# Row counts that are multiples of 16 in the transfers of a message-passing kernel, and 60 one-hot blocks in place of 58

## The chip, the cores and the metric

The kernel runs on one core of one Trainium2 chip. The core has a matrix engine (PE, TensorE), a vector engine (DVE), a scalar engine (ACT), GpSimd (POOL), a queue engine (SP) that only issues transfers here, and 16 DMA engines that the queues of SP, ACT and POOL share. The metric is the time of one execution on the device in microseconds, less being better.

## The reference

One layer of a graph network on 12,500 nodes with 32 features and 200,000 edges, the edges sorted by destination. For every edge the source row and the destination row go through a four-layer perceptron; the messages are averaged per destination node, added to x and normalised. The edge attributes are not used.

```
x_j = x[src];  x_i = x[dst]
h = relu(concat([x_i, x_j - x_i]) @ W1 + b1)      # 64 -> 64
h = relu(h @ W2 + b2)                             # 64 -> 128
h = relu(h @ W3 + b3)                             # 128 -> 64
m = h @ W4 + b4                                   # 64 -> 32
s, cnt = segment_sum(m, dst), segment_sum(1, dst) # over 12,500 nodes
out = layernorm(x + s / max(cnt, 1))
```

## The kernel before

The edges are cut into 196 blocks of 1,024 (`S_N`). Each block is one step of a pipeline: PE makes layer 1, ACT applies the relus, PE makes layers 2 and 3, turns the result and sums it into a window of nodes with a one-hot of the destinations that DVE builds. Layer 4 is applied once per node at the end.

The source rows of a block come in one of two ways. In a *gathered* block POOL issues eight indirect transfers of 128 rows each (L564), of rows of x for the first five blocks (`PLAIN`) and of rows of x that layer 1 has already been applied to (`z_rows`) for the others; PE only turns them (L859). POOL runs up to ten blocks ahead (`R`). In a *sorted* block (the first `SB` = 58 blocks of edges) no row is gathered: DVE builds one-hots of the sources (L1270) from lists that SP spreads over the partitions (`load_windows`, L467), and PE picks the rows out of all 12,500 nodes with 113 small matmuls (`selected_x`, L897). Those lists are sorted on DVE before (`merge`, L1143 and L1144), turned into windows by ACT (`window_sources`, L656), stored in DRAM by SP (`store_windows`, L458) and loaded again.

`STEPS` sets the order: 14 gathered steps, then from step 14 on one sorted step and two gathered steps in turn until the sorted blocks are used up (step 185), then gathered steps to the end (186 to 195). SP, ACT, PE and DVE each go through the steps in this order, in a loop of one pass for this input.

Ahead of the steps, in seven groups of 16 node columns (`YG`, `YC`), PE applies layer 1 to all nodes (L790), ACT and DVE split the result (L636, L637, L1062, L642, L1068), and SP stores it in DRAM: `z_rows` (L418) and `y_rows` (L420). The nodes lie as 125 partitions (`NP`) of 100 nodes. The buffers of a group are used again two groups later, so ACT waits at L634 and L635 for the stores of the group before last. POOL's gathers of `z_rows`, and the first step, wait for all of the stores.

Transfers whose partition count is not 128 are: the load of x by ACT (L608, 125 rows), the destinations of the gathered blocks (`dst_i`, L380, 68 rows) and their relative form (L424, `LP` = 69 rows), the stores of `z_rows` and `y_rows` (125), of the three parts of x (`x_rows`, L512, two pieces of 125 rows) that are loaded again as 98 blocks (`load_blocks`, L427), of the windows of sources (L458, 58 rows, eight pieces), the load of x once more for the end (L494, 125 rows), issued in the first step after the last sorted one and used by DVE two steps later (`centre_x`, a quarter of the columns in each of four steps), and the store of the result in eight chunks (L545, 125 rows).

Of the kernel before, what the change touches and what calls it, by code (L numbers as in the profile page):

```python
# [13 lines left out]
N, E = 12500, 200000  # L14
# [14 lines left out]
XP = 3 * D  # L29


SB = 58
HALVES = 64
GB = S_N - SB
B0 = SB * PE2
LP = GB // 2
LC = 2 * PE2
# [13 lines left out]
for n in range(S_N):  # L51
    k = (n - FIRST_SORTED) // PERIOD
# [40 lines left out]
YG = 7  # L93
NP = 125
# [3 lines left out]
CHUNKS = [(0, EDGE)] + [(EDGE + CH * n, CH) for n in range(6)] + [(NC - EDGE, EDGE)]  # L98
LAG = 2
XH = 2  # L100
# [12 lines left out]
def build(nc, x, src, dst, W1, b1, W2, b2, W3, b3, W4, b4, consts, bounds, out):  # L113
# [3 lines left out]
    with ctx:  # L117
# [53 lines left out]
        rel16 = part(region16, 0, (LC,))[0:LP, :]  # L171
        x_nat = part(region, ring, (NC * D,))[0:NP, :]
# [29 lines left out]
        x_parts = part(x_p, 0, (NC, 3, D))  # L202
# [7 lines left out]
        dst_i = part(sums_all, 2 * SBL * T, (LC,))[0:LP, :].bitcast(I32)  # L210
# [11 lines left out]
        z_new = [part(work, n * 5 * UE, (YC, H1))[0:NP, :, :] for n in range(2)]  # L222
        y_new = [part(work[:, :].bitcast(BF16), n * 10 * UE + 4 * UE, (YC, 3, H1))[0:NP, :, :, :] for n in range(2)]
# [66 lines left out]
        s_x2 = sem("x_in_once_more")  # L290
# [61 lines left out]

        def rows_stored(eng, rows):
            for n in range(2):
                eng.wait_ge(rows[n], 16 * len(range(n, YG, 2)))

        def layer3_copied(eng, s):

            if s < AHEAD - 2:
                eng.wait_ge(s_h3a, s + 1)  # L360
            else:
                eng.wait_ge(s_h3c, s + 3 - AHEAD)

        def piece(h):
            return slice(h * NC // XH, (h + 1) * NC // XH)
# [6 lines left out]
        def _(sp):  # L372
# [4 lines left out]
            sp.dma_start(src_i[0:FULL - fb * T, fb, :], tiled[fb * T:FULL, :]).then_inc(s_src, 16)  # L377
            sp.dma_start(src_i[FULL - fb * T:FULL - fb * T + 1, fb, 0:HALF], src[E - HALF:E].unsqueeze(0)).then_inc(s_src, 16)
            body = dst[B0:B0 + (LP - 1) * LC].rearrange("(p e) -> p e", e=LC)
            sp.dma_start(dst_i[0:LP - 1, :], body).then_inc(s_dst, 16)  # L380
            a = E - B0 - (LP - 1) * LC
            lastp = dst_i[LP - 1:LP, :]
            sp.dma_start(lastp[:, 0:a], dst[B0 + (LP - 1) * LC:E].unsqueeze(0)).then_inc(s_dst, 16)
# [31 lines left out]
            for g in range(YG):  # L415
                at, w = slice(g * YC, g * YC + width(g)), width(g)
                sp.wait_ge(s_znew, g + 1)
                sp.dma_start(z_rows.rearrange("(p c) f -> p c f", p=NP)[:, at, :], z_new[g % 2][:, 0:w, :]).then_inc(s_zst[g % 2], 16)  # L418
                sp.wait_ge(s_ylo, g + 1)
                sp.dma_start(y_rows[0:N, :, :].rearrange("(p c) k f -> p c (k f)", p=NP)[:, at, :],  # L420
                             y_new[g % 2][:, 0:w, :, :].rearrange("p c k f -> p c (k f)")).then_inc(s_yst[g % 2], 16)
                if g == 0:
                    sp.wait_ge(s_rel16, 1)
                    sp.dma_start(dst_rows[B0:B0 + LP * LC].rearrange("(p e) -> p e", e=LC), rel16).then_inc(s_dst_st, 16)  # L424
# [50 lines left out]
            def step(s):  # L475
                if is_sorted(s) and STEPS[s] + 1 < SB:
                    for c in range(CN - QN):
                        load_windows(STEPS[s] + 1, QN + c)
                if s + RX < S_N:
                    load_dst(s + RX)  # L480
                    load_rows(s + RX)
                if AHEAD <= s < SSTEP[0] - 1:
                    for c in range(3):
                        if 3 * (s - AHEAD) + c < CN:
                            store_windows(3 * (s - AHEAD) + c)
                if s == SSTEP[0] - 2:
# [9 lines left out]
            sp.wait_ge(s_dst_st, 16)  # L496
            sp.wait_ge(s_ypad, 16)
            rows_stored(sp, s_yst)
            load_first()
            for s in range(AHEAD):  # L500
                step(s)
                if s == 0:
                    sp.wait_ge(s_keys, 1)
                    for n, v in enumerate((bound_lo, bound_hi)):
                        sp.dma_start(v[0:SB, :], bounds[n, :].unsqueeze(0).to_broadcast([SB, PE2])).then_inc(s_bound, 16)
                if s == HALF_STEP:
                    sp.wait_ge(s_half, 1)
                    sp.dma_start(key0[0:SB, 0:UE], key0[HALVES:HALVES + SB, UE:PE2]).then_inc(s_across, 16)
                if s == PARTS_STEP:
                    for h in range(XH):  # L510
                        sp.wait_ge(s_lo, h + 1)
                        sp.dma_start(x_rows[0:N, :, :].rearrange("(p c) k f -> p c k f", p=NP)[:, piece(h), :, :],  # L512
                                     x_parts[0:NP, piece(h), :, :]).then_inc(s_xst, 16)
                if s == PARTS_STEP + 1:
                    sp.wait_ge(s_xst, (XH + 1) * 16)
# [26 lines left out]

            for n, (c0, w) in enumerate(CHUNKS):
                sp.wait_ge(s_y, n + 1)
                sp.dma_start(out.rearrange("(p c) f -> p c f", p=NP)[:, c0:c0 + w, :], zc[:, c0:c0 + w, :]).then_inc(s_out, 16)  # L545
            sp.wait_ge(s_out, 16 * len(CHUNKS))

        @block.gpsimd
        def _(pool):
# [55 lines left out]

        @block.scalar
        def _(act):
            act.dma_start(x_nat, x.rearrange("(p c) f -> p (c f)", p=NP)).then_inc(s_x, 16)  # L608
# [21 lines left out]
            def split_rows(g):  # L630
                for i in range(4):
                    act.wait_ge(s_zy4[i], g + 1)
                if g >= 2:
                    act.wait_ge(s_zst[g % 2], 16 * (g // 2))  # L634
                    act.wait_ge(s_yst[g % 2], 16 * (g // 2))  # L635
# [121 lines left out]
        def _(pe):  # L757
# [34 lines left out]
                        if t == width(g) // 4 - 1:  # L792
                            made.then_inc(s_zy4[i], 1)

            pe.wait_ge(s_x, 16)
            turn_x(0)
            pe.wait_ge(s_w1s, 1)
            for g in range(YG):
# [204 lines left out]
        def _(dve):  # L1003
# [17 lines left out]
                    nc.vector.tensor_copy(src_t[:, a:b], ps[:, k, 0:b - a]).then_inc(s_idx, 1)  # L1021

            def subtract_bases():
                dve.wait_ge(s_dst, 4 * 16)
# [267 lines left out]
            def build_onehot(s):  # L1292
                v, n = s % 2, STEPS[s]
                if s >= 2:
                    dve.wait_ge(s_agg, s - 1)
                if n == 0:
                    dve.wait_ge(s_maskc, 1)
                if s == 0:
                    dve.wait_ge(s_dst_st, 16)
# [66 lines left out]
            with dve.Fori(0, end, WIN) as off:  # L1366
# [3 lines left out]
                for s in range(AHEAD, S_N + 3):  # L1370
# [2 lines left out]
                        copy_masked()  # L1373
                    if SSTEP[-1] + 3 <= s < SSTEP[-1] + 3 + XQ:
                        if s == SSTEP[-1] + 3:
                            dve.wait_ge(s_x2, 16)
# [86 lines left out]
```

## Time and profile before

| | |
|---|---|
| median of 3 runs | 2545.24 us (2544.97 to 2545.98) |
| profiled execution, its own time | 2551.01 us |
| its span | 2549.2 us |
| mean granted TensorE clock | 0.803 |
| PE busy | 1782.1 us (70%) |
| DVE, ACT, POOL busy | 844.8, 634.2, 1093.8 us (33%, 25%, 43%) |
| moved by DMA | 300.61 MB |

Busy time is summed over instructions, and matmuls overlap, so a busy PE is not PE at its peak. "Idle before" in a row of the timeline is the time that the engine stood still ahead of that instruction, and behind the arrow stands what ended it; "remote" there means that the profile does not show who did, "issue" that nothing it shows was waited for.

### The profile page before, as it was taken

The numbers are of one execution on the slowest core, as the hardware profiler recorded it, in microseconds if no ns is written. First come the engines' busy times: TensorE is split into PE (matmuls) and PEld (weight loads), VectorE is DVE, ScalarE is ACT, GpSimd is POOL, SyncE is SP. The second block draws the span as 40 slices with busy tenths as digits, with TensorE's granted clock in tenths as the row PEclk, the third lists the DMA queues.
The fourth block names the chain that finished last, engine by engine and source line by source line (L and its number), as shares of the span: only waits on it lengthen the run. The fifth ranks groups of instructions, "written<-read, shape, count | busy, mean of one in ns | idle before, by whom it ended". The sixth has DMA issues, their size and how long they took to land.

```text
span 2549.2 us, 39560 instructions
## 1 busy us (share of the span) xinstructions
PE 1782.1 (70%) x13928; PEld 1173.7 (46%) x13928; DVE 844.8 (33%) x1777; ACT 634.2 (25%) x999; POOL 1093.8 (43%) x1123
## 2 busy tenths in 40 slices
PE   2133516777787777787777777777877778777887
PEld 2111303555454554555554555554555545555547
DVE  2342602333333333333333333332333333333352
ACT  2222314222222222222222222222222222222241
POOL 4175263444444444444444444444344444444402
PEclk9975756878878788878888878888788888887885
DMA  3221414444434444444444444443444443444310
GB/s 114 81 65 29 114 35 149 142 133 133 132 112 140 137 139 125 126 123 142 139 138 125 127 123 142 136 138 105 128 142 137 139 123 120 131 142 133 93 58 27
DMA packets 194466, 300.61 MB, mean 118 GB/s; under 512 B 83633, under 2 KB 90015, under 8 KB 193697
## 3 DMA queue, kind: packets, MB, share of 16 engines
q1 hardware_dynamic: 158439, 260.74, 32.3%
q0 software_dynamic: 35168, 35.43, 6.7%
q8 instruction: 116, 1.90, 0.3%
q10 hardware_dynamic: 658, 1.85, 0.2%
q14 instruction: 85, 0.70, 0.1%
HBM read 283.89 MB, written 13.87 MB: 117 GB/s over the span
## 4 chain that ended last, share of the span: by engine, by line
PE 41%; another core or an unknown queue 22%; issue 16%; DVE 9%; DMA 5%; ACT 3%; DVEq 3%; SPq 0%; POOL 0%; ACTq 0%; POOLq 0%
PE ps L897 21%; PE ps L921 5%; PE ps L929 3%; PE ps L949 3%; DVEq L1314 3%; PE ps L937 2%; PE ps L841 2%; PE ps L911 2%; PE ps L998 2%; DVE region L1270 2%; DVE region L1301 2%; PE ps L859 1%; DMA dstb<-dst_rows 1%; DMA y_rows<-work 1%
## 5 line engine op out<-in xcount | busy, mean ns | idle before, releaser
L564 POOL DMA_INDIRECT xj<-z_rows,src_t x1059 | 1038.2, 980 | 1293.4 <-PE ps L859 785.6
L897 PE MATMUL ps<-region,x_p 128*96 128x155 bf16 (+51 forms) x6554 | 611.4, 259 | 268.5 <-issue 238.0
L897 PEld LDWEIGHTS ps<-region,x_p 128*96 128x96 bf16 x6554 | 544.1, 162 | 395.4 <-issue 367.3
L1270 DVE TENSOR_SCALAR region<-region,cst 128x1629 bf16<-128x1629 int16 x464 | 274.0, 643 | 348.6 <-remote 295.1
L929 PE MATMUL ps<-work,w3s 128*64 128x512 f32 x784 | 311.5, 697 | 69.0 <-ACT work L683 38.5
L683 ACT ACTIVATE work<-ps,b2s 128x512 f32<-128x512 f32 x392 | 256.8, 685 | 205.7 <-remote 147.0
L1289 DVE COPY work<-ps 128x512 f32<-128x512 f32 x188 | 129.2, 687 | 504.0 <-remote 278.5
L921 PE MATMUL ps<-work,w2s 64*128 64x512 f32 x784 | 252.9, 726 | 45.5 <-ACT work L675 41.1
L690 ACT ACTIVATE work<-ps,b3s 128x512 f32<-128x512 f32 x196 | 134.7, 687 | 529.6 <-remote 468.4
L675 ACT ACTIVATE work<-ps,b1s 128x512 f32<-128x512 f32 x196 | 134.8, 688 | 507.7 <-PE ps L841 363.0
L937 PE MATMUL ps<-cst,work 128*128 128x128 f32 x784 | 138.3, 303 | 139.8 <-ACT work L690 99.3
L1316 DVE TENSOR_TENSOR sums<-sums,ps 65x42 f32 (+1 forms) x334 | 67.7, 203 | 361.3 <-remote 179.0
L952 PE MATMUL ps<-region,work 128*65 128x42 f32 x2208 | 177.3, 248 | 12.4 <-issue 6.6
L952 PEld LDWEIGHTS ps<-region,work 128*65 128x65 f32 x2208 | 175.8, 159 | 12.9 <-issue 11.5
L921 PEld LDWEIGHTS ps<-work,w2s 64*128 64x128 f32 x784 | 65.4, 204 | 237.0 <-ACT work L675 164.8
L937 PEld LDWEIGHTS ps<-cst,work 128*128 128x128 f32 x784 | 89.7, 150 | 178.0 <-ACT work L690 112.4
L664 ACT ACTIVATE work<-ps 96x512 bf16<-96x512 f32 x58 | 34.4, 593 | 491.5 <-PE ps L897 491.5
L929 PEld LDWEIGHTS ps<-work,w3s 128*64 128x64 f32 x784 | 61.4, 150 | 150.4 <-ACT work L683 84.4
L1280 DVE CAST work<-ps 96x512 bf16<-96x512 f32 x58 | 39.8, 687 | 247.5 <-PE ps L897 247.5
L859 PEld LDWEIGHTS ps<-cst,xj 128*128 128x128 f32 x552 | 59.8, 144 | 127.5 <-issue 127.5
L859 PE MATMUL ps<-cst,xj 128*128 128x128 f32 x552 | 93.6, 294 | 20.5 <-DVE work L1233 19.3
L841 PE MATMUL ps<-region,ywin 126*64 126x512 bf16 x508 | 93.1, 400 | 20.8 <-DVE region L1262 11.6
(156 smaller groups left out, 940.2 us busy)
## 6 DMA issues: line engine op xcount, KB each, us to landing
dstb<-dst_rows SPq DMA_DIRECT2D x196, 252.0 KB
region<-src_rows SPq DMA_DIRECT2D x116, 391.2 KB
region<-src_rows SPq DMA_DIRECT2D x58, 407.2 KB
region<-src_rows SPq DMA_DIRECT2D x58, 403.2 KB, 4.8
region<-src_rows SPq DMA_DIRECT2D x58, 376.2 KB
region<-src_rows SPq DMA_DIRECT2D x58, 375.8 KB, 3.7
region<-src_rows SPq DMA_DIRECT2D x58, 374.0 KB
region<-src_rows SPq DMA_DIRECT2D x58, 366.2 KB, 5.4
```

Of the source, the lines that this page charges most:

```text
L564: pool.indirect_dma_start(out=xj[:, u, j % UT, j // UT, 0:w], out_offset=None, in_=rows, in_offset=bass.IndirectOffsetOnAxis(ap=cols[:, j: ...
L675: nc.scalar.activation(h1[:, v, :], p_h1, ACT.Relu, bias=b1s[:, 0:1]).then_inc(s_r1, 1)
L683: nc.scalar.activation(h2[:, v, h, :], p_h2[:, h, :], ACT.Relu, bias=b2s[:, 0:1]).then_inc(s_r2[h], 1)
L690: nc.scalar.activation(h3[:, v, :], p_h3, ACT.Relu, bias=b3s[:, 0:1]).then_inc(s_r3, 1)
L841: added = nc.tensor.matmul(p_h1[h * H1:(h + 1) * H1, :], rows, pick[:, v, k, h * UE:(h + 1) * UE], start=False, stop=k == steps - 1, skip_ ...
L859: turned = nc.tensor.matmul(to[:, t * T:(t + 1) * T], xj[:, u, t, :, :].rearrange("p h f -> p (h f)"), ident, start=t == 0, stop=True, is_ ...
L897: chosen = nc.tensor.matmul(ps[0:XP, XBANK[h], lo - h * UE:hi - h * UE], xb[:, a, :], hot[:, q % QN, at + lo:at + hi], start=not begun[h], ...
L921: nc.tensor.matmul(p_h2[:, h, :], w2s[r:r + H1, :], h1[r:r + H1, s % 2, :], start=True, stop=True).then_inc(s_l2[h], 1)
L929: nc.tensor.matmul(p_h3[h * H3:(h + 1) * H3, :], w3s[:, :], h2[:, s % 2, h, :], start=True, stop=True).then_inc(s_l3, 1)
L937: turned = nc.tensor.transpose(p_ht[:, t * T:(t + 1) * T], h3[:, s % 2, t * T:(t + 1) * T], ident)
L952: summed = nc.tensor.matmul(p_agg[:, h * KN:(h + 1) * KN], h3t[:, v, t, h, :], onehot[:, v, j, 0:KN], start=t == 0, stop=t == UT - 1)
L1270: nc.vector.tensor_scalar(hot[:, q % QN, 0:CW[c]], spread[:, q % QE, 0:CW[c]], cst[:, C_PID:C_PID + 1], None, ALU.is_equal).then_inc(s_hot, 1)
```

## The change

Two things. `SB` goes from 58 to 60: with it the gathered blocks go from 138 to 136, `LP` from 69 to 68, the partitions that hold the sorted blocks from 58 to 60, and steps 188 and 191 are sorted steps. And every transfer of 125, 68 or 67 rows is issued as two: a multiple of 16 rows (112 or 64) and the rest (13, 4 or 3); the semaphore counts follow.

```diff
-SB = 58
+SB = 60
+        def even_rows(n):
+            return slice(0, n // 16 * 16), slice(n // 16 * 16, n)
...
-            sp.dma_start(dst_i[0:LP - 1, :], body).then_inc(s_dst, 16)
+            for rows in even_rows(LP - 1):
+                sp.dma_start(dst_i[rows, :], body[rows, :]).then_inc(s_dst, 16)
...
-                sp.dma_start(z_rows.rearrange("(p c) f -> p c f", p=NP)[:, at, :], z_new[g % 2][:, 0:w, :]).then_inc(s_zst[g % 2], 16)
+                for rows in even_rows(NP):
+                    sp.dma_start(z_rows.rearrange("(p c) f -> p c f", p=NP)[rows, at, :], z_new[g % 2][rows, 0:w, :])\
+                        .then_inc(s_zst[g % 2], 16)
...
-                    sp.wait_ge(s_block, CN * SB)
-                    sp.dma_start(x_nat, x.rearrange("(p c) f -> p (c f)", p=NP)).then_inc(s_x2, 16)
+                    for rows in even_rows(NP):
+                        sp.dma_start(x_nat[rows, :], x.rearrange("(p c) f -> p (c f)", p=NP)[rows, :]).then_inc(s_x2, 16)
```

In the same manner the stores of `y_rows` (L420), of the relative destinations (L424), of `x_rows` (L512) and of the result (L545), and ACT's load of x (L608). The stores of the windows (L458), of the sorted destinations (L519) and the copy L508 are not split; their row count is `SB`. Waits change only in their counts (`2 * 16` for `16`, `5 * 16` for `4 * 16`, `2 * XH + 1` for `XH + 1`).

## Rows read from the trace of the kernel before

**Rows 1.** Stretches: us, busy time of each engine, granted clock, DMA share, GB/s
```profile
10.00:15.00 5.00, 0.00 (x0) 0.00 (x0) 0.00 (x0) 3.42 (x2) 0.00 (x0) 1.00 0.32 133
110.00:115.00 5.00, 0.81 (x8) 0.51 (x8) 2.69 (x3) 3.00 (x3) 0.00 (x0) 1.00 0.32 132
408.00:410.00 2.00, 0.00 (x0) 0.00 (x0) 0.00 (x0) 1.15 (x2) 0.00 (x0) 1.00 0.20 58
414.00:416.00 2.00, 1.08 (x14) 1.11 (x15) 0.65 (x1) 0.00 (x0) 0.00 (x0) 0.50 0.74 296
```

**Rows 2.** Timeline, the start: us, duration, engine, line, what, idle before
```profile
2.03 12.62 SPq L378 DMA_DIRECT2D sums<-in_src  x1
21.65 1.16 ACT L619 ACTIVATE sums<-sums 128x1152 f32<-128x1152 int32 x1 [8.23 <-DMA sums<-in_src]
26.06 1.12 POOL L564 DMA_INDIRECT xj<-in_x,src_t  x1 [24.69 <-DVE src_t L1021]
```

**Rows 3.** Timeline, the groups of node columns and their stores
```profile
77.09 0.94 POOL L564 DMA_INDIRECT xj<-in_x,src_t  x1 [0.30 <-issue]
83.81 1.02 ACT L636 ACTIVATE work<-ps 125x1024 f32<-125x1024 f32 x1 [37.84 <-remote]
91.11 1.02 ACT L636 ACTIVATE work<-ps 125x1024 f32<-125x1024 f32 x1 [3.02 <-PE ps L790]
...
120.06 0.38 ACT L636 ACTIVATE work<-ps 125x256 f32<-125x256 f32 x1 [5.43 <-DMA y_rows<-work]
122.11 0.27 SPq L420 DMA_DIRECT2D y_rows<-work  x1
131.79 0.95 POOL L564 DMA_INDIRECT xj<-z_rows,src_t  x1 [53.75 <-DMA z_rows<-work]
133.51 0.07 DVE L1233 MEMSET work<- 128x16 f32 x1 [11.42 <-DMA y_rows<-work]
```

**Rows 4.** Timeline, the parts of x stored and loaded again
```profile
261.02 1.67 SPq L512 DMA_DIRECT2D x_rows<-x_p  x2
...
281.62 0.85 SPq L427 DMA_DIRECT2D x_p<-x_rows  x1
...
296.60 0.49 DVE L1262 TENSOR_SCALAR region<-dstb,node_off 126x1024 bf16<-126x1024 int16 x1 [2.46 <-DMA dstb<-dst_rows]
```

**Rows 5.** Timeline, the last store of windows and the first load
```profile
402.84 0.24 SPq L458 DMA_DIRECT2D src_rows<-region  x1
...
410.08 4.37 SPq L467 DMA_DIRECT2D region<-src_rows  x8
```

**Rows 6.** Timeline, DVE's one-hots of sorted blocks, POOL's last gather
```profile
445.83 0.84 DVE L1301 TENSOR_TENSOR region<-iota_s,dst_rel 128x672 f32<-128x672 f32 x1
...
2407.45 0.85 DVE L1301 TENSOR_TENSOR region<-iota_s,dst_rel 128x672 f32<-128x672 f32 x1
2408.65 0.95 POOL L564 DMA_INDIRECT xj<-z_rows,src_t  x1 [0.31 <-issue]
2427.30 0.85 DVE L1301 TENSOR_TENSOR region<-iota_s,dst_rel 128x672 f32<-128x672 f32 x1
```

**Rows 7.** Timeline, PE inside one sorted block, and in the last gathered steps
```profile
1500.73 0.68 PE L897 MATMUL ps<-region,x_p 128*96 128x153 bf16 x4 [1.04 <-issue]
1503.59 6.80 PE L897 MATMUL ps<-region,x_p 128*96 128x12 bf16 x69 [0.86 <-issue]
...
2463.67 0.65 PE L859 MATMUL ps<-cst,xj 128*128 128x128 f32 x4
2468.18 0.66 PE L859 MATMUL ps<-cst,xj 128*128 128x128 f32 x4
```

**Rows 8.** Timeline, x loaded once more and its first use
```profile
2424.13 0.28 SPq L494 DMA_DIRECT2D region<-in_x  x1
...
2440.65 0.99 DVE L1320 TENSOR_REDUCE xmean<-region 125x25 f32<-125x800 f32 x1 [7.73 <-DMA region<-in_x]
2441.67 0.18 DVE L1321 TENSOR_SCALAR xmean<-xmean 125x25 f32<-125x25 f32 x1
```

**Rows 9.** SP's waits: line, waited for, us in total, times, longest
```profile
SPq L117 <- DMA out<-region: 6.5, 1, 6.5
```

More of the change, by code:

```diff
@@ L354, in rows_stored @@
             for n in range(2):
-                eng.wait_ge(rows[n], 16 * len(range(n, YG, 2)))
+                eng.wait_ge(rows[n], 2 * 16 * len(range(n, YG, 2)))
         def layer3_copied(eng, s):
@@ L417, in _ @@
                 sp.wait_ge(s_znew, g + 1)
-                sp.dma_start(z_rows.rearrange("(p c) f -> p c f", p=NP)[:, at, :], z_new[g % 2][:, 0:w, :]).then_inc(s_zst[g % 2], 16)
+                for rows in even_rows(NP):
+                    sp.dma_start(z_rows.rearrange("(p c) f -> p c f", p=NP)[rows, at, :], z_new[g % 2][rows, 0:w, :])\
+                        .then_inc(s_zst[g % 2], 16)
                 sp.wait_ge(s_ylo, g + 1)
-                sp.dma_start(y_rows[0:N, :, :].rearrange("(p c) k f -> p c (k f)", p=NP)[:, at, :],
-                             y_new[g % 2][:, 0:w, :, :].rearrange("p c k f -> p c (k f)")).then_inc(s_yst[g % 2], 16)
+                for rows in even_rows(NP):
+                    sp.dma_start(y_rows[0:N, :, :].rearrange("(p c) k f -> p c (k f)", p=NP)[rows, at, :],
+                                 y_new[g % 2][rows, 0:w, :, :].rearrange("p c k f -> p c (k f)")).then_inc(s_yst[g % 2], 16)
                 if g == 0:
                     sp.wait_ge(s_rel16, 1)
-                    sp.dma_start(dst_rows[B0:B0 + LP * LC].rearrange("(p e) -> p e", e=LC), rel16).then_inc(s_dst_st, 16)
+                    for rows in even_rows(LP):
+                        sp.dma_start(dst_rows[B0:B0 + LP * LC].rearrange("(p e) -> p e", e=LC)[rows, :], rel16[rows, :])\
+                            .then_inc(s_dst_st, 16)
             def load_blocks(rows):
@@ L493, in step @@
                     sp.wait_ge(s_block, CN * SB)
-                    sp.dma_start(x_nat, x.rearrange("(p c) f -> p (c f)", p=NP)).then_inc(s_x2, 16)
-            sp.wait_ge(s_dst_st, 16)
+                    for rows in even_rows(NP):
+                        sp.dma_start(x_nat[rows, :], x.rearrange("(p c) f -> p (c f)", p=NP)[rows, :]).then_inc(s_x2, 16)
+            sp.wait_ge(s_dst_st, 2 * 16)
             sp.wait_ge(s_ypad, 16)
@@ L511, in _ @@
                         sp.wait_ge(s_lo, h + 1)
-                        sp.dma_start(x_rows[0:N, :, :].rearrange("(p c) k f -> p c k f", p=NP)[:, piece(h), :, :],
-                                     x_parts[0:NP, piece(h), :, :]).then_inc(s_xst, 16)
+                        for rows in even_rows(NP):
+                            sp.dma_start(x_rows[0:N, :, :].rearrange("(p c) k f -> p c k f", p=NP)[rows, piece(h), :, :],
+                                         x_parts[rows, piece(h), :, :]).then_inc(s_xst, 16)
                 if s == PARTS_STEP + 1:
-                    sp.wait_ge(s_xst, (XH + 1) * 16)
+                    sp.wait_ge(s_xst, (2 * XH + 1) * 16)
                     load_blocks(x_rows[0:NROT, :, :])
@@ L544, in _ @@
                 sp.wait_ge(s_y, n + 1)
-                sp.dma_start(out.rearrange("(p c) f -> p c f", p=NP)[:, c0:c0 + w, :], zc[:, c0:c0 + w, :]).then_inc(s_out, 16)
-            sp.wait_ge(s_out, 16 * len(CHUNKS))
+                for rows in even_rows(NP):
+                    sp.dma_start(out.rearrange("(p c) f -> p c f", p=NP)[rows, c0:c0 + w, :], zc[rows, c0:c0 + w, :])\
+                        .then_inc(s_out, 16)
+            sp.wait_ge(s_out, 2 * 16 * len(CHUNKS))
         @block.gpsimd
@@ L607, in _ @@
         def _(act):
-            act.dma_start(x_nat, x.rearrange("(p c) f -> p (c f)", p=NP)).then_inc(s_x, 16)
+            for rows in even_rows(NP):
+                act.dma_start(x_nat[rows, :], x.rearrange("(p c) f -> p (c f)", p=NP)[rows, :]).then_inc(s_x, 16)
             act.dma_start(cst[:, :], consts).then_inc(s_cst, 16)
@@ L633, in split_rows @@
                 if g >= 2:
-                    act.wait_ge(s_zst[g % 2], 16 * (g // 2))
-                    act.wait_ge(s_yst[g % 2], 16 * (g // 2))
+                    act.wait_ge(s_zst[g % 2], 2 * 16 * (g // 2))
+                    act.wait_ge(s_yst[g % 2], 2 * 16 * (g // 2))
                 nc.scalar.activation(four(z_new[g % 2], g), of_group(slice(0, H1), g), ACT.Copy).then_inc(s_znew, 1)
@@ L793, in make_rows @@
                             made.then_inc(s_zy4[i], 1)
-            pe.wait_ge(s_x, 16)
+            pe.wait_ge(s_x, 2 * 16)
             turn_x(0)
@@ L1023, in subtract_bases @@
             def subtract_bases():
-                dve.wait_ge(s_dst, 4 * 16)
+                dve.wait_ge(s_dst, 5 * 16)
                 nc.vector.tensor_reduce(base_p[:, :], dst_i.rearrange("p (h e) -> p h e", h=UP), AX.X, ALU.min)\
@@ L1298, in build_onehot @@
                 if s == 0:
-                    dve.wait_ge(s_dst_st, 16)
+                    dve.wait_ge(s_dst_st, 2 * 16)
                 nodes, w = (iota_s, WIN) if n < SB else (iota_g, KN)
@@ L1375, in _ @@
                         if s == SSTEP[-1] + 3:
-                            dve.wait_ge(s_x2, 16)
+                            dve.wait_ge(s_x2, 2 * 16)
                         centre_x(s - SSTEP[-1] - 3)
```

## The prediction

> **What bounds the kernel now.** I read the times of stretches first. While a transfer of 125 rows is the only large one, as x in the first microseconds and y at 110, the DMA share stands at 0.32 with 132 to 133 GB/s [rows 1]. 0.32 of 16 engines is five, at 26 GB/s each. With stores of 58 rows the share is 0.20 at 58 GB/s, which is two engines at that rate and a rest of gathers; with loads over 128 partitions it is 0.74 and 296 GB/s, with the ramp inside the stretch [rows 1]. So a transfer seems to be dealt out in equal shares of whole rows: 125 = 5 x 25, 58 = 2 x 29, 128 = 16 x 8. The change turns 125 into 112 = 16 x 7 and 13, 69 into 64 and 4, and, unsaid, every 58 into 60 = 15 x 4.
>
> Then I ask with the timeline where such a transfer ends a wait on the path. The reader is to see six places: the start [rows 2], the groups of node columns [rows 3], the parts of x [rows 4], the windows [rows 5], the second load of x [rows 8] and the end [rows 9]. Between 446 and 2407 us none does. There the time is made by PE's order of steps. From one sorted one-hot to the next but 55 is (2407.45 - 445.83) / 56 = 35.03 us for one sorted and two gathered steps [rows 6]. When POOL has issued its last gather, at 2408.65, the next such period takes 2427.30 - 2407.45 = 19.85 us, and a gathered step alone 2468.18 - 2463.67 = 4.51 us [rows 6, 7]. In the period before, 16 gathers were issued. PE's small matmuls show why: while POOL gathers they come in threes and fours with gaps of about 1 us ("issue"), and after its last gather of the burst 69 of them pass in 6.80 us [rows 7]. A gather thus costs PE about (35.03 - 19.85) / 16 = 0.95 us although PE waits for no data. A gathered block costs 4.51 + 8 x 0.95 = 12.1 us, a sorted one 19.85 - 2 x 4.51 = 10.8 us.
>
> **The change part by part.** The sum is made against the profiled execution's 2551.0 us (span 2549.2), which is 5.8 above the median of the runs; that difference is kept.
>
> (a) Start. ACT's copy of the sources begins at 21.65 after 8.23 us of idle that a load of sources ended; SP stood 12.62 us in the issue of the last of these [rows 2], as long as x (1.6 MB at 133 GB/s is 12.0 us) holds the first five engines. On 16 engines x takes about 4 us. The copy can then start when ACT's own work ends, 8.2 us earlier; everything behind it, POOL's first gather at 26.06 too, moves with it. Value 8.2; bounds 0 (another engine's load is late instead) and 8.2.
>
> (b) The long wait. ACT waits 37.84 us for PE's third group, until 83.81, and POOL's 40th gather ends at 78.03 [rows 3]. PE's work for that group is there early in the trace; its result becomes visible only once POOL has stopped, the same effect as in rows 7. I take the wait as tied to the end of the gathers: they start 8.2 us earlier, so it ends 8.2 us earlier, and nothing is added to (a). Bounds: 0 gained (it hangs on something fixed, and (a) is lost), or the group gets through before the gathers bite, 28 us gained beyond (a).
>
> (c) Groups three to six and the stores. Without a wait for a store a group takes 91.11 - 83.81 = 7.30 us. At that pace the last group starts at 91.11 + 3 x 7.30 = 113.0 in place of 120.06 [rows 3]: 7.0 gained, up to 10 since the last group is a quarter as wide. After the last store is issued at 122.11 DVE waits to 133.51, 11.4 us, for 1.25 MB and more of backlog on five engines; on 16 at 300 to 400 GB/s the backlog is gone and about 3.5 us are left: 7.9 gained. POOL's start at 131.79 hangs on the same stores. Together 15.5; bounds 13 and 18. What is late next is the pace of ACT, DVE and PE in a group.
>
> (d) Parts of x. The two stores issued at 261.02 (2.4 MB, 18 us at 132 GB/s) hold SP until 281.62; the load behind them delays DVE's list at 296.60 by 2.46 us [rows 4]. With 16 engines SP gets on some 9 us earlier and that idle goes: 2.5; bounds 0 and 4.
>
> (e) Windows. From the last store's issue to the first load is 410.08 - 402.84 = 7.24 us [rows 5] for two stores of 170 KB on two engines. On 15 engines 2.5 us or so: 4.7 gained, and PE's first sorted block, which waits for it, moves. No row shows a transfer of 60 rows, so the bounds are 0 and 4.9. I take 4.5, as all three row counts in rows 1 follow the same division.
>
> (f) Two blocks change their kind. From step 182 on before: 35.03 + 19.85 + 8 x 4.51 = 91.0 us. After, the last gather is issued one period earlier, so four periods run free of gathers, and two gathered steps remain: 4 x 19.85 + 2 x 4.51 = 88.4. That is 2.5 gained; I take 2, since three free periods in a row are not in the trace. Bounds: 2.5 gained, and 43 lost, if the 35.03 us belong to the sorted block and not to the gathers (two periods of 35.03 for six steps of 4.51).
>
> (g) x once more. Issued at 2424.13, it ends DVE's idle of 7.73 us at 2440.65 [rows 8], and PE stands behind DVE. On 16 engines it should be there in 6 to 7 us, before DVE asks (8.8 us after the issue): 7.7 gained. But with the last sorted step at 191 the four quarters of centring (0.99 + 0.18 + 0.99 us and links, 2.2 us each [rows 8]) fall in steps 194 to 197, where PE has little left and DVE sets the pace. I charge 2.2 for the last, which stands right ahead of the final sums, and 2.5 for the three others: net 3.0; bounds 0 and 7.
>
> (h) The end. SP waits 6.5 us for the last stores of the result [rows 9], some 0.55 MB of them queued on five engines. On 16, with one issue of 0.3 us more, 3.5 are left: 3.0; bounds 1 and 4.
>
> (i) At nothing: 27 more issues on SP and one on ACT, 0.25 to 0.3 us each, lie beside waits of SP for groups and steps, except the one in (h); if SP were late, each pair would cost 0.3. No wait is added, only counts change.
>
> Sum: 8.2 + 15.5 + 2.5 + 4.5 + 2 + 3 + 3 = 38.7, so 2512.3 for a profiled execution and 2506.5, say 2507, for the median.
>
> The rows give the number of engines only by their share. The Trainium skill, "DMA: Bandwidth & Descriptors", section on why a DMA increments its semaphore by 16, has the rule: the largest number up to 16 that divides both sides' outer dimension. The trace agrees for 125 (0.32) and 58 (0.20). By it 60 rows go over 15 engines and the rest of 13 over 13; without it, were 60 rows left on two, the sum would be 34.2.
>
> Another page speaks against the change. "SBUF — State Buffer", section on the setup-cost knee: each transfer pays about 2 us whatever its size, so one large transfer is preferred. An estimate by that page, if the second of each pair were paid in full behind the first in (c), (d) and (h), is 6 us less gain, 2513. No row here shows two halves of one transfer.
>
> **The rivals.**
> 1. *A sorted block has its own price.* The mechanism is PE in steps 188 to 193: if a period of sorted and gathered steps takes 35.03 us whether or not POOL gathers, six tail steps of 4.51 become two such periods, 43 us more, and the transfers' 36.7 are eaten: 2551, slower. It decides from a period of about (36.7 + 27.1) / 2 = 31.9 us. For it speaks that 55 periods show 35 and only one shows 19.85; against it the gaps in rows 7, which end with the gather. 5%.
> 2. *The long wait is not tied to POOL's first gather.* It stays at its place, (a) is lost: 2515. What speaks for it is "remote", the profile names no releaser. 15%.
> 3. *The wait shrinks.* Groups one to three finish ahead of most gathers, as the first load of destinations is early too; half of the 28 us goes: 2493. Against it, both PE and POOL hang on the same list of sources and move together. 13%.
> 4. *The change doesn't spread the transfers.* If 0.32 came from the shape of a row, not the count of rows, 112 rows are as slow as 125, only (f) and the late centring are left: -2 + 4.7, 2548. The 128-row loads at 296 GB/s speak against it. 4%.
>
> **How the numbers follow.** The forecast has 63%, its own range 2498 to 2516. Rival 2 reaches to 2520 with small losses in (f) and (g), rival 3 to 2485. With these the range 2487 to 2522 leaves out the rest, rivals 1 and 4, and part of rival 3. 0.2% (5 us) is what a measurement can tell from no change here: faster 0.92, the same 0.04 (rival 4 and a part of 1), slower 0.04.
>
> **What would show it.** After: ACT's copy of the sources near 13.5; a DMA share well over 0.5 in the groups' stores and ACT's L636 every 7.3 us; POOL's second series of gathers and DVE's memset near 108 to 110; L427 within 11 us of L512; L467 within 3 us of the last L458; no idle on x before the centring; three periods near 20 us at the end, and the others unchanged at 35. It is wrong if the periods at the end are over 30 us, if POOL's second series begins after 118, or if what is won by 133 us is lost again by 446.

## The result, and the profile after

The changed kernel takes 2499.97 us (median of 4 runs, 2498.25 to 2500.88), the kernel before in the same series 2545.17 (4 runs, 2544.97 to 2545.98): a ratio of 0.9821, 95% interval 0.9804 to 0.9838, 45.2 us less. The forecast was 2507, 38 us less, with a range of 2487 to 2522.

The profiled execution after is 2498.25 us with a span of 2496.4, the lowest of its runs; the one before lay 5.8 above its median. Of the 52.8 us between the two profiles 7.6 are therefore not in the medians.

Page of after: busy time by engine, then the chain that ended last, by engine. The second view has the same chain in before.
```profile
span 2496.4 us, 40078 instructions
PE 1777.5 (71%) x14162; PEld 1176.8 (47%) x14162; DVE 856.4 (34%) x1795; ACT 638.0 (26%) x1001; POOL 1076.1 (43%) x1107
...
PE 44%; another core or an unknown queue 22%; issue 16%; DVE 9%; ACT 4%; DVEq 3%; DMA 0%; ACTq 0%; SPq 0%; POOL 0%; POOLq 0%
```
```profile
PE 41%; another core or an unknown queue 22%; issue 16%; DVE 9%; DMA 5%; ACT 3%; DVEq 3%; SPq 0%; POOL 0%; ACTq 0%; POOLq 0%
```
No engine does noticeably less than before (POOL alone lost 16 gathers), so most of the time came out of waits. DMA has 0% of the chain in place of 5%.

Stretches of after, to be held against [rows 1]: x alone at the start, then a store of `y_rows` with the next one of `z_rows`. (A share a little over 1 is possible because the durations of packets are added up.)
```profile
3.00:6.00 3.00, 0.00 (x0) 0.00 (x0) 0.00 (x0) 0.00 (x0) 0.00 (x0) 1.00 1.01 320
84.00:87.00 3.00, 0.00 (x0) 0.00 (x0) 1.61 (x2) 1.71 (x3) 0.00 (x0) 0.50 0.86 259
```
The DMA share is 1.01 and 0.86 where it was 0.32. From 3 to 6 us 16 packets of x are under way at a time, in before 5, and the last packet of x ends at 9.0 us, in before at 16.7. The rate at the full share is 320 GB/s, less than 16 times the 26 of [rows 1], so x takes 7 us and not the 4 of the prediction. That cost nothing, since the copy waits for ACT's own work.

Timeline of after, the start, to be held against [rows 2].
```profile
2.02 3.42 SPq L382 DMA_DIRECT2D sums<-in_src  x1
...
13.87 1.16 ACT L634 ACTIVATE sums<-sums 128x1152 f32<-128x1152 int32 x1
...
18.26 1.12 POOL L578 DMA_INDIRECT xj<-in_x,src_t  x1 [16.89 <-DVE src_t L1036]
```
The issue that held SP for 12.62 us takes 3.42, and the copy and the first gather come 7.8 us earlier.

Timeline of after, the groups of node columns and their stores, for [rows 3].
```profile
69.18 0.95 POOL L578 DMA_INDIRECT xj<-in_x,src_t  x1 [0.30 <-issue]
76.12 1.02 ACT L651 ACTIVATE work<-ps 125x1024 f32<-125x1024 f32 x1 [39.34 <-remote]
83.42 1.02 ACT L651 ACTIVATE work<-ps 125x1024 f32<-125x1024 f32 x1 [3.02 <-PE ps L805]
...
102.02 0.38 ACT L651 ACTIVATE work<-ps 125x256 f32<-125x256 f32 x1 [0.32 <-PE ps L805]
...
106.83 1.15 SPq L428 DMA_DIRECT2D y_rows<-work  x2
109.11 0.94 POOL L578 DMA_INDIRECT xj<-z_rows,src_t  x1 [38.98 <-DMA z_rows<-work]
110.05 0.07 DVE L1248 MEMSET work<- 128x16 f32 x1 [4.47 <-DMA y_rows<-work]
```
The long wait is still there (39.34 us), shifted by 7.7 with the gathers. The 5.43 us on a store ahead of the last group are gone (0.32, on PE), and DVE's wait behind the last store is 4.47 in place of 11.42. POOL's second series starts 22.7 us earlier, DVE's memset 23.5.

PE's last matmuls of the third group, before and after; they end at 56.05 and 48.69, 28 and 27 us ahead of ACT's start.
```profile
55.27 0.78 PE L790 MATMUL ps<-w1zy,x_t 32*125 32x128 f32 x2 [0.33 <-issue]
```
```profile
47.60 1.09 PE L805 MATMUL ps<-w1zy,x_t 32*125 32x128 f32 x3 [1.74 <-issue]
```

Timeline of after, the parts of x, the windows, then x once more: [rows 4], [rows 5] and [rows 8].
```profile
236.60 4.84 SPq L524 DMA_DIRECT2D x_rows<-x_p  x4
248.38 0.87 SPq L437 DMA_DIRECT2D x_p<-x_rows  x1
...
370.73 4.70 SPq L468 DMA_DIRECT2D src_rows<-region  x2
377.26 4.83 SPq L477 DMA_DIRECT2D region<-src_rows  x8
...
2407.25 0.79 SPq L505 DMA_DIRECT2D region<-in_x  x2
2416.45 0.99 DVE L1335 TENSOR_REDUCE xmean<-region 125x25 f32<-125x800 f32 x1 [0.37 <-DMA region<-in_x]
```
The load of the parts follows its stores' first issue after 11.8 us (20.6 before; 11 was forecast). From the end of the last window store's issue to the first load it is 377.26 - 375.43 = 1.8 us (7.0 before), and 0.37 us of the 7.73 on x remain.

Timeline of after, POOL's last gather and one-hots of the last five sorted blocks, for [rows 6].
```profile
412.44 0.85 DVE L1316 TENSOR_TENSOR region<-iota_s,dst_rel 128x672 f32<-128x672 f32 x1
...
2329.16 0.85 DVE L1316 TENSOR_TENSOR region<-iota_s,dst_rel 128x672 f32<-128x672 f32 x1
2330.37 0.95 POOL L578 DMA_INDIRECT xj<-z_rows,src_t  x1 [0.31 <-issue]
2350.16 0.85 DVE L1316 TENSOR_TENSOR region<-iota_s,dst_rel 128x672 f32<-128x672 f32 x1
...
2390.62 0.85 DVE L1316 TENSOR_TENSOR region<-iota_s,dst_rel 128x672 f32<-128x672 f32 x1
2410.47 0.85 DVE L1316 TENSOR_TENSOR region<-iota_s,dst_rel 128x672 f32<-128x672 f32 x1
```
The four periods behind the last gather take 21.0, 20.2, 20.2 and 19.9 us. The 55 before it have a median of 34.75 (34.92 in before). The first one-hot's lead of 445.83 - 412.44 = 33.4 us has so grown to 43.2 by step 179.

Stretches from the one-hot of step 14 to that of step 179, before and after:
```profile
445.83:2372.35 1926.52, 1491.47 (x12049) 982.65 (x12047) 639.99 (x1321) 467.40 (x715) 862.62 (x881) 0.82 0.44 131
```
```profile
412.44:2329.16 1916.72, 1482.05 (x12047) 979.99 (x12045) 641.61 (x1322) 470.83 (x715) 861.72 (x881) 0.82 0.43 132
```
PE stands idle for 435.0 and 434.7 us of them, the same. The 9.8 us are matmul time: 1491.5 and 1482.1 us for the same work. By the trace's records of the granted clock, PE was at the lower of its two levels (1.2 GHz) for 693 and 676 us.

SP's last wait in after, for [rows 9]: 1.3 us in place of 6.5.
```profile
SPq L117 <- DMA out<-region: 1.3, 1, 1.3
```

### The profile page after: what moved, and what is told of

Same layout as the page of the kernel before. It is cut to its first block, busy times and chain, and to the rows that moved or that the text cites. A ratio compares the mean times of both kernels' runs of the same rounds, so it can differ in the third digit from the quotient of the medians.

```text
span 2496.4 us, 40078 instructions
## 1 busy us (share of the span) xinstructions
PE 1777.5 (71%) x14162; PEld 1176.8 (47%) x14162; DVE 856.4 (34%) x1795; ACT 638.0 (26%) x1001; POOL 1076.1 (43%) x1107
## 4 chain that ended last, share of the span: by engine, by line
PE 44%; another core or an unknown queue 22%; issue 16%; DVE 9%; ACT 4%; DVEq 3%; DMA 0%; ACTq 0%; SPq 0%; POOL 0%; POOLq 0%
PE ps L912 22%; PE ps L936 5%; PE ps L944 4%; PE ps L964 3%; DVEq L1329 3%; PE ps L952 2%; PE ps L856 2%; PE ps L926 2%; PE ps L1013 2%; PE ps L874 2%; DVE region L1285 2%; DVE region L1316 1%; ACT work L690 1%; DVE region L1159 1%
## 5 line engine op out<-in xcount | busy, mean ns | idle before, releaser
L578 POOL DMA_INDIRECT xj<-z_rows,src_t x1043 | 1020.6, 979 | 1240.6 <-PE ps L874 751.5
L912 PE MATMUL ps<-region,x_p 128*96 128x127 bf16 (+54 forms) x6780 | 613.6, 256 | 257.8 <-issue 233.0
L1285 DVE TENSOR_SCALAR region<-region,cst 128x1629 bf16<-128x1629 int16 x480 | 283.7, 644 | 340.3 <-remote 309.1
L967 PEld LDWEIGHTS ps<-region,work 128*65 128x65 f32 x2176 | 173.6, 160 | 15.0 <-issue 14.9
```

The costliest lines, as they stand in the source:

```text
L578: pool.indirect_dma_start(out=xj[:, u, j % UT, j // UT, 0:w], out_offset=None, in_=rows, in_offset=bass.IndirectOffsetOnAxis(ap=cols[:, j: ...
L912: chosen = nc.tensor.matmul(ps[0:XP, XBANK[h], lo - h * UE:hi - h * UE], xb[:, a, :], hot[:, q % QN, at + lo:at + hi], start=not begun[h], ...
L967: summed = nc.tensor.matmul(p_agg[:, h * KN:(h + 1) * KN], h3t[:, v, t, h, :], onehot[:, v, j, 0:KN], start=t == 0, stop=t == UT - 1)
L1285: nc.vector.tensor_scalar(hot[:, q % QN, 0:CW[c]], spread[:, q % QE, 0:CW[c]], cst[:, C_PID:C_PID + 1], None, ALU.is_equal).then_inc(s_hot, 1)
```

## The experiments

They ran on four chips, here A to D, none of which showed the periods of 35 us of the first series. The kernel before took 1610.6 to 1611.9 us on each of them (medians of 9 or 10 runs), not 2545. Which chip the first series ran on is not on record. Differences between runs on different chips are taken over the kernel before on the same chip.

**On chip A: the kernel before again, and each half of the change alone.** The first has no edit. The second is the change with

```diff
-SB = 60
+SB = 58
```
and the third the kernel before with the reverse, no transfer split. The fourth is the change with splits at multiples of 15:

```diff
-            return slice(0, n // 16 * 16), slice(n // 16 * 16, n)
+            return slice(0, n // 15 * 15), slice(n // 15 * 15, n)
```

> The kernel before, unchanged, for a second trace. Between the 17th and the 173rd one-hot of DVE (L1301) the changed kernel gained 9.6 us (33.6 to 43.3 us ahead) that no step of the prediction names. Theory N: the first profiled execution of before was itself slow there (its own time is 2551.0, the median 2545.2); the new trace then shows that stretch 4 to 10 us shorter than the first one's 1820.1 us. Rival S: the changed kernel is really faster there; the new trace shows 1820 within 2 us.

Measured: 1611.67 us in one run (before: 1610.92, 10 runs). Timeline of this run, PE around one sorted block while POOL gathers.
```profile
501.40 6.47 PE L897 MATMUL ps<-region,x_p 128*96 128x26 bf16 x113
```
All 113 small matmuls pass without a gap in 6.47 us. In [rows 7] they came in threes and fours with gaps of about 1 us. The median period is 20.24 us, not 34.92, and the mean granted clock 0.936, not 0.803. The stretch of the same 55 periods, steps 14 to 179:
```profile
297.32:1413.55 1116.23, 1112.85 (x12049) 768.86 (x12045) 635.45 (x1321) 456.49 (x715) 863.07 (x831) 1.00 0.73 225
```
PE is busy for 20.2 of a period's 20.3 us here and its clock is never at the lower level. In the first series a period has 27.1 us of matmuls for the same work and 7.9 of idle, at a clock of 0.82. So of the 14.7 us between the two about half are gaps, and the other half are matmuls that take longer at the lower clock.

What the run was meant to tell apart, whether the 9.6 us in the middle belong to the change or to a long first profile of before, it could not, since it had no period of 35 us. Neither theory is shown.

> The split transfers alone, SB stays 58 (the whole change but its first line). By the prediction's terms the start, the groups, the parts of x, the end and the second load of x are gained (8.2 + 15.5 + 2.5 + 3.0 and 7.7 for the load, as the centring stays where PE has work): 37 us, 2508. The gap from the last store of windows (58 rows) to the first load stays at 7.2 us, since 58 rows still go over two engines. Rival (the row count of the windows doesn't matter, all of it comes from less traffic): the gap shrinks to 3 us as in the changed kernel.

Measured: 1574.26 us (5 runs), ratio 0.9770 (0.9756 to 0.9784), 36.7 us less. POOL's second series starts at 77.22, in the kernel before at 102.24. From there POOL's 1,058 gathers to the last take 8.9 us less, and what follows them 2.5 us less. The time of 2508 can't be held against a chip without the periods of 35 us. The gap behind the last store of windows stays long (7.8 us, views at the fourth kernel), as the theory had it.

> Two more sorted blocks alone, no transfer split. Theory: windows on 15 engines gain 4.5, the blocks 2, the second load of x (still 125 rows) stalls DVE again and the centring lies late, 5 lost; but the destinations are now one transfer of 67 rows, a prime, 549 KB on one engine at 26 GB/s, about 21 us in place of 5: DVE's first reduction (L1025) is late by some 15 us, of which the wait for PE's third group (until 83.8) covers all. Time 2540 to 2546. Rival 1 of the prediction (a sorted block costs 12 us more than the tail's gathered steps gain): 2570 or more, with periods of 35 us at the end.

Measured: 1614.78 us, ratio 1.0027 (1.0015 to 1.0039): slower. With 60 sorted blocks the destinations lie in 67 rows before the last. DVE's waits in the first 150 us, and POOL's first gather of `z_rows`:
```profile
DVE base_p L1025 <- DMA sums<-in_dst: 18.1, 1, 18.1
```
```profile
120.38 0.94 POOL L564 DMA_INDIRECT xj<-z_rows,src_t  x1 [42.64 <-DMA z_rows<-work]
```
In the kernel before, with 68 rows, DVE waits 1.0 us there and POOL goes on at 102.24. So the 60 blocks alone lose 18.1 us at the start. POOL's last gather is at 1519.87 all the same, 3.8 earlier than in the kernel before, as it has 16 gathers less; but what follows takes 6.8 us longer. Without the split this half costs 4 us. The theory had the late destinations right (18.1 us, 15 expected), but here no long wait covers them. The 67 packets of 8,192 bytes start one behind the other, 0.3 us apart, as on a single engine at 26 GB/s.

> The changed kernel with 15 in place of 16: 125 rows go as 120 and 5, 68 as 60 and 8, 67 as 60 and 7. Theory (a transfer goes over the largest number of engines up to 16 that divides its rows: 15 and 5): within 2 us of the changed kernel, 2500, and POOL's second series of gathers again at 109 to 110. Rival (a multiple of 16 is what counts): the 120-row stores are slow, the second series of gathers starts after 115, 2508 or more.

Measured: 1559.84 us, ratio 0.9685 (0.9671 to 0.9700), against 0.9653 and 0.9661 for the change on chips B and D: 4 to 5 us worse, where at most 2 were expected. POOL's second series starts at 78.68, there at 76.0, so the 120-row stores are not slow and the rival fell; the loss is there from the start, as the last packet of x ends 1.8 us later (10.8, in after 9.0) and POOL's first gather is at 21.07, not 18.4 to 18.8. Timelines of the windows on 58 rows (the second kernel) and on 60 (this one).
```profile
216.87 4.61 SPq L468 DMA_DIRECT2D src_rows<-region  x2
229.28 4.24 SPq L477 DMA_DIRECT2D region<-src_rows  x8
```
```profile
218.11 4.70 SPq L468 DMA_DIRECT2D src_rows<-region  x2
224.64 4.26 SPq L477 DMA_DIRECT2D region<-src_rows  x8
```
From the end of the last store's issue to the first load it is 7.8 us with 58 rows and 1.8 with 60, and while the one-hots of steps 4 to 8 come at the same times within 0.2 us, that of step 11 comes 4.5 us earlier and that of step 14 still 4.3. This is term (e). The windows are not split in either kernel, nor are the destinations of the third, so it is the row count that decides and not that there are two transfers.

The Trainium skill ("DMA: Bandwidth & Descriptors", the section on why a DMA increments its semaphore by 16) lets a transfer use the largest number of engines up to 16 that divides the outer dimension of both its sides. By that 67 rows have one engine, 60 have 15 and 58 two. The traces agree for 67 rows (0.55 MB in packets one behind the other, a wait of 18.1 us) and for 58 against 60 (gaps of 7.8 and 1.8 us). For 120 rows, 15 packets of x are under way at a time in this kernel, where 112 rows had 16; for 60 rows the number itself is not shown.

**On chip B: the change, the stores of the groups, and POOL.**

> The changed kernel. On the chip of the last four runs PE's small matmuls run undisturbed beside POOL's gathers (113 in 6.5 us, a period of 20.2 us), on the chip of the first two traces they don't (35.0). Theory: the gathers' price for PE belongs to the chip, so on the second chip this kernel takes what the split by 15 took, 1557 to 1563, against 1611 before; on the first it is 2500. In either case the gain is 45 to 52 us. Rival: the second chip's gain came from the split by 15, and this one gains less than 45.

Measured: 1556.05 us (1553.76 to 1557.76), before 1611.9 on the same chip: ratio 0.9653 (0.9634 to 0.9672), 55.9 us less. The rival fell; the time lies 1 us under the range of the theory and the gain 4 us over its 45 to 52. The groups' timeline, ACT, has no long wait.
```profile
28.13 1.02 ACT L651 ACTIVATE work<-ps 125x1024 f32<-125x1024 f32 x1 [1.27 <-PE ps L805]
35.44 1.02 ACT L651 ACTIVATE work<-ps 125x1024 f32<-125x1024 f32 x1 [3.02 <-PE ps L805]
...
61.34 0.38 ACT L651 ACTIVATE work<-ps 125x256 f32<-125x256 f32 x1 [0.32 <-DMA y_rows<-work]
```
The chain of this run, by engine, from its page:
```profile
POOL 64%; issue 21%; DVE 6%; PE 5%; DMA 1%; DVEq 1%; ACT 1%; SPq 0%; POOLq 0%; ACTq 0%
```
POOL is the bound here: from its 41st gather (76.02) to its last (1467.28) it needs 1391.3 us for 1,042 intervals, 1.335 each, 21.4 for the 16 of a period in which PE needs 20.23. PE lives on the ten blocks of lead until they are spent.

> The changed kernel with the stores of z_rows and y_rows whole again (125 rows, five engines). Theory, step (c) of the prediction: 13 to 18 us slower than the changed kernel on either chip, POOL's gathers of z_rows (the 41st on) begin that much later. Rival: the other splits make room on the engines and these stores matter less, under 8 us.

```diff
-                for rows in even_rows(NP):
+                for rows in (slice(0, NP),):
```
(both stores of a group, counts back to 16). Measured: 1578.01 us, ratio 0.9792 (0.9768 to 0.9817): the stores alone are worth 22 us, more than the 13 to 18 expected. ACT's timeline and POOL's:
```profile
63.35 1.02 ACT L651 ACTIVATE work<-ps 125x1024 f32<-125x1024 f32 x1 [6.32 <-DMA y_rows<-work]
74.36 1.02 ACT L651 ACTIVATE work<-ps 125x1024 f32<-125x1024 f32 x1 [6.72 <-DMA y_rows<-work]
84.14 0.38 ACT L651 ACTIVATE work<-ps 125x256 f32<-125x256 f32 x1 [5.49 <-DMA y_rows<-work]
```
```profile
97.48 0.94 POOL L578 DMA_INDIRECT xj<-z_rows,src_t  x1 [24.52 <-DMA z_rows<-work]
```
Where the groups follow each other without the long wait, the stores on five engines run late from an earlier group on. The rival (under 8 us) fell.

> The changed kernel, but POOL stops after 16 gathers until the last group's y rows are made. Where gathers hold up PE (period 35): the long wait before the third group, 39 us, ends at once, groups follow each other every 7.3 us, and the first step begins at about 80 in place of 110: 20 to 30 us faster than the changed kernel. Rival there: the wait has another cause and stays, 0 gained. Where they don't (period 20): nothing waits for the pause, and POOL, which is the path there, starts its 17th gather some 35 us late: 25 to 35 us slower.

```diff
+                if g == 2:
+                    pool.wait_ge(s_ylo, YG)
```
(in POOL's loop of first gathers, behind 16 of them). Measured: 1568.95 us, ratio 0.9732 (0.9709 to 0.9756), 12.9 us above the change. POOL's first gather of `z_rows` is 21.1 us later than without the pause (97.11), its last 13.4. The first one-hot is not earlier (96.98 against 97.25): here the gathers don't hold up PE, and the pause only costs. The miss is one of size: 25 to 35 us were expected, but POOL's 17th gather starts 24.5 us late, not 35, and 8 of them are made up by the last gather.

> The changed kernel with four of the eight gathers of each gathered block left out from the 16th gathered block on (the rows of the other 512 edges are those of an earlier block, so the sums are not the reference's); PE does all its matmuls. Where gathers hold up PE: 8 gathers fewer a period, 35.0 - 8 x 0.95 = 27.4 us a period, about 2040 in all. Where they don't: the period stays at PE's 20.2, and only the end, where eight gathered steps wait for POOL at 10 us each, gains: 30 to 45 us. Rival (a period is PE's own work on both chips): 35.0 stays.

```diff
-            return PT if g < GB - 1 else LAST
+            return (PT if g < 15 else PT // 2) if g < GB - 1 else LAST
```
The kernel leaves out half of the gathers from the 16th gathered block on. Measured: 1534.32 us in one run, 21.7 below the change; 30 to 45 were expected. Its chain by engine:
```profile
PE 84%; DVE 6%; ACT 3%; DMA 2%; issue 2%; DVEq 1%; SPq 1%; POOL 0%; ACTq 0%; POOLq 0%
```
PE takes the path over and the period stays at 20.2. So where PE runs undisturbed, POOL's gathers make this kernel 22 us longer than PE would, no more. (With half the gathers there is also less traffic; one run doesn't separate the two.)

**On chip C: the first load of x.**

> The changed kernel with ACT's first load of x as one transfer of 125 rows again; everything else as changed. It isolates term (a). Theory A (the term as forecast): ACT's copy of the sources and POOL's first gather begin some 7 us later than in the kernel with the whole change (first gather about 26 in place of 18.8), and since POOL's stream of gathers sets the path where gathers don't hold up PE, the whole kernel takes 6 to 8 us more than the change. Theory B (the start is absorbed, because the first gathered rows wait for the stores of the groups anyway): POOL's 40th gather ends 7 us later, but its 41st begins no later than in the changed kernel, or by less than 3 us, and the time is within 3 us of the change. Where gathers hold up PE (a kernel before of about 2545 us), A expects the wait before the third group to end 7 to 8 us later too, and rival 2 of the prediction expects that wait to end at the same time as in the changed kernel.

```diff
-            for rows in even_rows(NP):
+            for rows in (slice(0, NP),):
                 act.dma_start(x_nat[rows, :], x.rearrange("(p c) f -> p (c f)", p=NP)[rows, :]).then_inc(s_x, 16)
```
Measured: 1565.28 us, ratio 0.9718 (0.9704 to 0.9732), against 0.9653 and 0.9661 for the change on chips B and D: 9 to 10 us, a little over the 6 to 8 expected. SP's timeline, then ACT's:
```profile
2.02 11.90 SPq L382 DMA_DIRECT2D sums<-in_src  x1
```
```profile
23.43 1.16 ACT L634 ACTIVATE sums<-sums 128x1152 f32<-128x1152 int32 x1 [10.08 <-DMA sums<-in_src]
```
SP is held in the issue again, the first gather starts at 27.82 (18.84 on chip B), the 41st at 85.48 (76.02), the last 10.8 us later. Theory A holds: nothing between absorbs it. How the wait before the third group would have moved the run can't say, as there is none here.

**On chip D: the change, x once more, the stores of the result.** The edits are the same replacement of `even_rows(NP)`, at the second load of x or at the stores of the result, with the counts halved.

> The changed kernel once more, as the measure for the two kernels beside it. If gathers don't hold up PE here (before near 1611 us): 1553 to 1558 us. If they do (before near 2545 us): about 2500 us, which would say that the condition comes and goes with the chip.

Measured: 1556.92 us (1552.64 to 1558.44), before 1611.71, ratio 0.9661 (0.9642 to 0.9680).

> The changed kernel with only the load of x for the end as one transfer of 125 rows again. It isolates the gain in term (g). Theory A (the term as forecast): DVE waits for x ahead of the centring by some 7 us, PE stands behind DVE, 5 to 8 us more than the change. Theory B (where POOL's gathers set the path of the last steps, 10 us each, DVE has spare time): DVE still waits some 7 us for x, but the last sorted one-hots and the end of the kernel move by less than 2 us.

Measured: 1558.25 us (1557.07 to 1561.24), ratio 0.9679 (0.9661 to 0.9696). Neither theory had this: DVE does not wait for x at all. SP's timeline and DVE's.
```profile
1455.22 0.28 SPq L505 DMA_DIRECT2D region<-in_x  x1
```
```profile
1474.71 0.24 DVE L1331 TENSOR_TENSOR sums<-sums,ps 65x84 f32 x1 [1.45 <-PE ps L964]
1474.87 0.98 DVE L1335 TENSOR_REDUCE xmean<-region 125x25 f32<-125x800 f32 x1
```
The steps at the end wait for gathers and take up to 14 us here, so 19.7 us lie between the issue and the first use. The 1.3 us of the medians are less than what the two ranges tell apart. Term (g), where the last steps are short, is not tested by this run.

> The changed kernel with only the stores of the result as whole transfers of 125 rows again. It isolates term (h). Theory A (as forecast): SP's last wait is some 5 us longer and the end of the kernel 3 to 4.5 us later than in the changed kernel, whatever bounds the steps. Theory B (the end hangs on the last chunk's own transfer, not on those queued before it): less than 1.5 us.

Measured: 1558.18 us (1557.16 to 1562.97), ratio 0.9679 (0.9659 to 0.9698). SP's last wait:
```profile
SPq L117 <- DMA out<-region: 5.7, 1, 5.7
```
It is 1.3 in the change. From DVE's last cast (L1412) to the end of the span it is 1558.1 - 1495.0 = 63.1 us, in the change 1555.7 - 1497.2 = 58.6. Of these 4.5, 1.0 lie in a later start of PE behind the cast and 3.5 behind POOL's last instruction, where the stores end. The 1.0 is scatter: in the two traces of the changed kernel on chips B and D PE starts 5.7 and 4.5 us behind the cast. The medians differ by 1.3 only, within their ranges. By the trace it is theory A at the lower end of its 3 to 4.5; by the run times it isn't shown.

## Why the prediction was right

The time came out 7 us under the forecast, inside its own range for the likeliest case. The terms of the sum, 38.7 us, measure 40.2 between the two first profiles. Another 12.6 us between these profiles are in no term; 7.6 of the 52.8 are not in the medians. By its steps, with the leads of after over before:

- **(a) start, 8.2:** 7.8 in the trace. The run with x whole again shows the cause, and 9 to 10 us of total time where POOL is the bound.
- **(b) the long wait tied to POOL's gathers:** the third group's lead is 7.7, and that of POOL's 40th gather 7.9; in both traces ACT goes on 6 us after that gather's end. Rival 2 (it stays) and rival 3 (it shrinks) both fell on that series. The other chips fit the tie: where gathers don't hold up PE the wait doesn't exist. It is no proof, since the pause of POOL could not be tried where the wait is. That PE's result becomes visible only once POOL has stopped is argued, not shown.
- **(c) groups and stores, 15.5:** 23.5 - 7.8 = 15.7 at DVE's memset, 22.7 - 7.8 = 14.9 at POOL. The 22 us measured with whole stores belong to a start without the long wait. From the memset to step 6 the lead grows by another 1.7, which is in no term.
- **(d) and (e), 2.5 and 4.5:** from step 6 to step 7 the lead grows from 25.2 to 27.8, 2.6 for (d), and by step 12 to 33.3, 5.6 for (e), over its bound of 4.9. That the row count of the windows does this is shown by the second and the fourth kernel of chip A.
- **(f) two blocks, 2, and (g) x once more, 3.0:** from the one-hot of step 179 to that of 195 it is 99.4 us after and 105.0 before, 5.6 gained; then the late centring takes 1.5 back up to DVE's last cast (the lead falls from 48.8 to 47.3). 4.1 together against 5; no run parts them where the periods of 35 us are. The free periods are 21.0 to 19.9, so rival 1 (35 for any sorted block) fell. The sum for (f) begins at step 179, not at 182 as it says.
- **(h) the end, 3.0:** 7.4 - 3.0 = 4.4 from POOL's last instruction to the end of the span, just above the bound of 4. The start of the final matmuls, another 1.0 sooner behind the cast, is scatter, as chips B and D show. The second issue of each pair hides beside the steps of the normalisation, and 1.3 us remain for the last chunk's transfer where I had left 3.5.
- **(i) issues at nothing:** the second issue of a pair took 0.3 to 1.1 us, once 2.9 (the last piece of `x_rows`), and in the groups, where most of them are, ACT keeps its 7.3 us. The Trainium skill prefers one large transfer because each pays about 2 us ("SBUF — State Buffer", the section on the setup-cost knee); the prediction's estimate from that page was 6 us less gain. The trace shows no such price for pairs that run side by side: (c), (d) and (h) came out at or above their terms.
- **Not in the sum:** 9.8 us between steps 14 and 179, 0.18 per period. PE's idle is the same in both, so no wait got shorter there. PE was at the lower clock for 17 us less; by the two stretches with and without the periods of 35 us (379 us more of matmuls for 693 at 1.2 GHz) that is worth 9.3 us, an estimate. Why the clock differed is open, and one profile of each kernel doesn't show that it belongs to the change. On chips B and D that stretch took 1121.8 and 1125.5 us after the change against 1116.2 on chip A before it, so it gained nothing there.

The weak step of the prediction is its first reading: "a gather costs PE 0.95 us" was read from 55 periods of one trace and taken for the kernel's nature. As a difference of periods it forecast the end rightly, but it is not one cost: only about half of it is PE standing still, and the rest is the lower granted clock. On four chips both are absent. That the changed kernel was measured under the same condition was luck for the number 2507.

On those chips the same change gains 55.9 and 54.8 us instead of 45.2. The splits alone gain 36.7. The sum without (e), (f) and the late centring is 36.9, an agreement that is partly luck: 25.0 us lie at the start, 8.9 in POOL's own gathers and 2.5 at the end, and there is no wait on x. The other 18 to 19 are for two blocks less to gather, close to 16 x 1.335 = 21.4 us of POOL's path. So (f), 2 in the first series, is next to the groups' stores (22) the largest term on chips A to D, and for another reason: POOL's own time, not PE's.

Still open: why PE's issue is slowed in the first series alone, whether POOL's gathers cause it, and whether it belongs to a chip or passes. The time of all 4 runs of each kernel in that series shows it. In the trace of before, 154 of PE's 179 us of idle between 500 and 1300 us lie beside running gathers, which fill 59% of that time; on chip A gathers run through the whole stretch and PE has no such idle.

## What to carry to other kernels

Look for DMA shares that stand at a low fraction while a large transfer runs alone, and divide its row count: 125, 58 and 67 rows used five, two and one of 16 engines. A multiple of 16 and the rest as a second transfer cost nothing that these traces show where the issuing queue has time; a multiple of 15 was 4 to 5 us worse over the whole kernel. When a size parameter is changed, recompute every row count that follows from it: 68 to 67 rows cost 18 us at the start here, 58 to 60 gained 4.3 to 5.6. A price read from one trace ("a gather costs PE 1 us") holds for that condition; look at the granted clock and at busy and idle time apart before you name the cause, and say what the change gives if the condition is absent.

## What the runs showed of the hardware

- The same kernel took 2545 us in one series and 1611 in later ones on four chips. In the first, small matmuls came with gaps of about 1 us while POOL gathered, the granted clock stood at 0.82 over these periods, and a wait for PE of 38 us ended only 6 us after the gathers did. In the later ones 113 of them ran in 6.47 us beside the gathers, at a granted clock of 1.00.
- The engines that share a transfer follow from its row count: 125 rows had a DMA share of 0.32, 112 and 13 rows one of 1.01; 67 rows made DVE wait 18.1 us where 68 made it wait 1.0.
- A transfer on few engines also holds the queue that issues later ones: SP stood 11.9 to 12.6 us in one issue behind x as 125 rows, 3.4 to 3.9 with 112 and 13, and 5.1 with 120 and 5.
- A gather of 128 rows takes POOL 0.94 us and 0.30 to the next at best, 1.335 from one to the next in the mean over a kernel.
